# Transformer block on one core: second feed-forward product as one 512-column product per rows tile, with its sums in four PSUM banks

## The reference

```python
h = _layernorm(x, ln3_g, ln3_b)
p = h @ ff_w1 + ff_b1                       # 256 -> 2048
a, gate = (p[..., :D_FF], p[..., D_FF:])    # 1024 each
h = a * jax.nn.gelu(gate, approximate=False) @ ff_w2 + ff_b2
return h + x
```

## Time and profile before

| | us |
|---|---|
| median of 3 runs (lowest, highest) | 1708.18 (1707.97, 1708.85) |
| span of the profiled execution, first to last instruction | 1706.1 |
| PE busy in the span | 1697.1 (99%) |
| DVE busy | 1467.8 (86%) |
| ACT busy | 1186.1 (70%) |
| POOL busy | 1086.0 (64%) |

### The profile page before, as it was taken

The page is one execution under the profiler, slowest core; times in us unless marked ns, Lnnn a source line. Parts: engine busy times, 40 slices in busy tenths (PEclk is TensorE's granted clock), DMA queues, the critical chain, the costliest instruction groups (busy, mean ns, idle before and its releaser), DMA issues.

```text
span 1706.1 us, 42969 instructions
## 1 busy us (share of the span) xinstructions
PE 1697.1 (99%) x13628; PEld 1661.4 (97%) x13628; DVE 1467.8 (86%) x3184; ACT 1186.1 (70%) x3246; POOL 1086.0 (64%) x1812
## 2 busy tenths in 40 slices
PE   9999999999999999999999999999999999999999
PEld 8999999999999999999999999999999998888888
DVE  8888988888888888899999999999999998666665
ACT  7777777777777777777788877777877776222222
POOL 7787777766666666687777877777777666122211
PEclk9999999999999999999999999999999999999999
DMA  7777777676666566677777777776666663212110
GB/s 215 192 183 185 178 183 177 172 179 163 154 155 155 151 161 158 168 180 179 187 193 193 195 193 177 183 180 167 169 168 169 167 165 83 62 50 71 63 42 25
DMA packets 286432, 263.99 MB, mean 155 GB/s; under 512 B 102016, under 2 KB 246528, under 8 KB 286208
## 3 DMA queue, kind: packets, MB, share of 16 engines
q1 hardware_dynamic: 232416, 248.12, 57.0%
q10 hardware_dynamic: 53792, 13.12, 3.6%
HBM read 70.40 MB, written 24.90 MB: 56 GB/s over the span
## 4 chain that ended last, share of the span: by engine, by line
PE 96%; DVE 1%; POOL 1%; SPq 1%; DMA 1%; ACT 1%; issue 0%; ACTq 0%; POOLq 0%; DVEq 0%
PE QKB L356 20%; PE PVB L415 14%; PE PTB L370 13%; PE WOP L395 10%; PE VB L317 9%; PE S L304 7%; PE S L303 7%; PE PTB L944 5%; PE S L944 5%; PE QKB L960 3%; PE VB L960 3%; DMA PT<-in_L_xattn_sa_wq_dram 0%; DMA RX<-QKS 0%; ACT PT L522 0%; DVE NM L633 0%
## 5 line engine op out<-in xcount | busy, mean ns | idle before, releaser
L522 ACT ACTIVATE PT<-S,NM 128x256 f32<-128x256 f32 x1024 | 471.1, 472 | 180.6 <-DVE NM L633 179.8
L615 DVE TENSOR_TENSOR PL<-PTB,PH 128x512 fp32r<-128x512 f32 x512 | 349.7, 684 | 90.4 <-ACT PH L543 86.2
L835 POOL TENSOR_TENSOR ON<-ON,RB 128x256 f32<-128x256 f32 x256 | 188.4, 736 | 277.3 <-DVE ON L653 262.4
L543 ACT ACTIVATE PH<-PTB 128x1024 fp32r<-128x1024 f32 x256 | 263.2, 1028 | 102.0 <-PE PTB L370 98.6
L633 DVE TENSOR_REDUCE NM<-S 128x2 f32<-128x512 f32 x512 | 325.9, 677 | 0.2
L370 PE MATMUL PTB<-IDN,PT 128*128 128x128 f32 x2048 | 265.9, 273 | 0.2
L303 PE MATMUL S<-RX 128*128 128x256 f32 x1012 | 253.8, 283 | 0.0
L304 PE MATMUL S<-RX 128*128 128x256 f32 x1012 | 253.7, 283 | 0.0
L370 PEld LDWEIGHTS PTB<-IDN,PT 128*128 128x128 f32 x2048 | 229.5, 140 | 0.9 <-DVE PL L615 0.8
L395 PE MATMUL WOP<-WO,OT 128*128 128x256 f32 x1536 | 226.0, 283 | 0.0
L653 DVE TENSOR_TENSOR ON<-PVB,ON 64x256 f32<-64x256 f32 x512 | 213.3, 417 | 3.5
(11 more groups left out here) (145 smaller groups left out, 3141.5 us busy)
## 6 DMA issues: line engine op xcount, KB each, us to landing
RX<-QKS SPq DMA_DIRECT2D x506, 192.0 KB, 2.9
RX<-QKS SPq DMA_DIRECT2D x506, 128.0 KB, 2.8
RB<-denominators SPq DMA_DIRECT2D x512, 64.0 KB, 2.6
out_dram<-XR SPq DMA_DIRECT2D x32, 256.0 KB, 2.7
rows<-XN SPq DMA_DIRECT2D x24, 256.0 KB, 2.5
rows<-HF SPq DMA_DIRECT2D x23, 256.0 KB, 2.5
XR<-in_x_dram SPq DMA_DIRECT2D x16, 256.0 KB, 3.6
denominators<-RDT SPq DMA_DIRECT2D x256, 16.0 KB
```

Source lines behind the costliest of these rows:

```text
L522: last = e.activation(PT[:, c % 2, j * S:(j + 1) * S], S1[:, i, qt * S:(qt + 1) * S], ACT.Exp, bias=NM[:, j:j + 1], accum_out=DEN[:, c % 2 ...
L543: e.activation(PH[:, s % 2, :], PTB[:, :, :].rearrange("p i n -> p (i n)"), ACT.Copy) \
L615: e.tensor_tensor(PL[:, cols], PTB[:, i, :], PH[:, s % 2, cols].bitcast(F32), ALU.subtract).then_inc(a.dve_pl, 1)
```

## The change

In chunks 1 to 7 the first two passes of the second product become one: the stationary operand is the high gated rows, the moving operand the high and the low weights side by side (512 columns). The result is twice as wide, so each of the four row tiles has a whole bank: the left 256 columns hold the high sums, the right ones the low sums. The third pass (low rows, high weights) is added to the left 256. The four banks are the former `QKB`, `VB`, `PVB` and `WOP`, now slices of one tensor `OUTB`. Chunk 0 stays as it was. For each half VectorE makes two additions to the residual rows: left columns, then, after a wait for it, right columns.

```diff
-        QKB = pb("QKB", [P, 512])
-        VB = pb("VB", [P, 512])
+        OUTB = pb("OUTB", [P, 4, 512])
+        QKB, VB, PVB, WOP = (OUTB[:, n, :] for n in range(4))
         S1 = pb("S1", [P, 2, 512])
         PTB = pb("PTB", [P, 2, 512])
-        PVB = pb("PVB", [P, 512])
-        WOP = pb("WOP", [P, 512])
...
+        def w2_both(f):
+            return WA[:, 4 + f // 4, :, (f % 4) * D:(f % 4 + 1) * D]
...
                     if f == 0 and t % 2 == 0:
                         sl.wait(e, fs.dve_xo, s, 1, PAIRS // 2 if t == 0 else 0)
+                    if s >= PAIRS:
+                        if s == PAIRS and t == 0:
+                            e.wait_ge(a.dve_ad, ATT)
+                            e.wait_ge(a.dve_xo, 2 * B)
+                        if s == PAIRS and t == 1:
+                            e.wait_ge(fs.dve_xo, PAIRS)
+                        high, low = (FH[:, s % 2, hp, t * P:(t + 1) * P] for hp in range(2))
+                        e.matmul(OUTB[:, t, :].rearrange("p (w n) -> p w n", w=2), high, w2_both(f), start=f == 0,
+                                 stop=False, skip_group_check=True)
+                        last = e.matmul(OUTB[:, t, 0:D], low, w2(f, 0), start=False, stop=f == PAIRS - 1,
+                                        skip_group_check=True)
+                        continue
                     for n, (hp, wp) in enumerate(((0, 0), (0, 1), (1, 0))):
...
-                    e.tensor_tensor(XR[:, cols], OB[h][:, :], XR[:, cols], ALU.add) \
-                        .then_inc(fs.dve_xo, PAIRS // 2)
+                    if chunk == 1:
+                        e.tensor_tensor(XR[:, cols], OB[h][:, :], XR[:, cols], ALU.add) \
+                            .then_inc(fs.dve_xo, PAIRS // 2)
+                        continue
+                    x = XR[:, cols].rearrange("p (t n) -> p t n", t=TT)
+                    y = OUTB[:, TT * h:TT * (h + 1), :].rearrange("p t (w n) -> p t w n", w=2)
+                    e.tensor_tensor(x, y[:, :, 0, :], x, ALU.add).then_inc(fs.dve_xh, 1)
+                    e.wait_ge(fs.dve_xh, 2 * (chunk - 2) + h + 1)
+                    e.tensor_tensor(x, y[:, :, 1, :], x, ALU.add).then_inc(fs.dve_xo, PAIRS // 2)
```

More of the change, by code:

```diff
@@ L868, in __init__ @@
                 self.dve_xo = sem("dve_xo_f")
+                self.dve_xh = sem("dve_xh_f")
                 self.pl_ve = sem("pl_ve_f")
```

## The result

The changed kernel takes 1713.88 us (median of 6 runs, 1713.52 to 1714.93) against 1708.43 for the one before, measured beside it (6 runs): +5.4 us, ratio 1.0033, 95% interval 1.0021 to 1.0044, that is +3.6 to +7.5 us. It is slower by more than 0.2%, by a narrow margin at the lower end. The forecast was +3.3 and 1711.5, and its range ended at 1713.6. Of the 2.4 us between 1711.5 and 1713.88, 0.25 are the kernel before, which measures 1708.43 here and stood at 1708.18 when the forecast was made. The profiled execution has a span of 1712.3, 6.2 above before.

What follows compares the result with a forecast made beforehand. PE was taken as the bound, busy 99% and never waiting in the changed stretch. Merges -2.8, boundaries +4.9 and the end +1.2 sum to +3.3 on 1708.18, 1711.5 us, with an 8-in-10 range of 1709.0 to 1713.6.

Steps and rivals of the forecast that it cites:

- Merged products: In the second product, one 512-column product replacing two of 256 saves 0.013 us per tile, -2.8 us over 54 steps.
- I take 0.013, the value nearest to the steady rows: Saving per merge in us, near 0.227 against 0.239 from trace streams of 512-column and 256-column products.
- The lower bound: For the merged products: with all 512s at 0.231 to 0.236 us, the gain is 0.004 per merge, -0.9 in all.
- The sign that the prediction set for this term: The prediction falls if a slot inside a chunk isn't within 0.02 of 4.13 us.
- Chunk boundaries: At six boundaries, into chunks 2 to 7, PE stops 0.82 us for DVE's additions: +4.9 us, bounds +4.5 to +5.4.
- dependent DVE instructions follow each other 0.03 after the end: At a chunk boundary, the gap in us taken between each half's left addition and the right one waiting for it.
- The end: At the kernel's end, the last four additions chain and end later: +1.2 us, 1.0 to 1.4.
- No cost elsewhere: New bank addresses, semaphore, one-off waits and first boundary's extra waits cost nothing; no second delay on DVE.
- the merged product saves less than its share: Rival for the second product: at 0.004 us per merge the time is 1713.4, slower by over 0.2%; chance 0.16.
- The boundaries don't stop PE: Rival at chunk boundaries: no stop, 1706.6 us, chance 0.05; with the larger saving 1703.7, chance 0.04.
- the larger saving: Rival for the second product: merges save 0.020 us per tile and 0.026 per slot, -5.7, 1708.6 us; chance 0.18.

Runs made afterwards that it cites:

- experiment 3: Changed kernel without VectorE's second addition per half, so the right columns are left out in chunks 1 to 7: 1705.70 us, ratio 0.9990 against before.
- experiment 6: Changed kernel with a slot's four 512-column products first and its four 256-column ones behind, in 48 slots: 1712.89 us, ratio 1.0030 against before.
- experiment 7: Changed kernel with the wide product's moving operand as 512 neighbouring columns of high weights in place of high and low ones: 1713.55 us in one run.
- Experiment 5: Changed kernel with left columns of both halves added first, then right columns of both: 1711.69 us, ratio 1.0023 against before.
- experiment 2: Changed kernel with each wide product made as two products of 256 columns again: 1715.12 us, ratio 1.0039 against before.
- experiment 4: Changed kernel with the second product of a chunk's first step made later at six boundaries: 1707.26 us, ratio 0.9997 against before.
- experiment 8: Changed kernel with grouped second products, late ones at the boundaries, and the last chunk in the old form: 1705.59 us, ratio 0.9989 against before.
- experiment 1: Kernel before with only the PSUM bank addresses of the change: 1707.80 us, ratio 1.0002 against before.

## Why the prediction was wrong

The mechanism was right: a gain on every slot, a stop at six boundaries, and a longer end. Each of the three terms was sized too kindly, and the errors added up: +3.3 was forecast, and +5.8 is the sum of what they measured in the traces (+5.4 between the medians).

- **Merged products: -2.8 forecast, -1.8 measured** (experiment 3). The step that failed is "I take 0.013, the value nearest to the steady rows". The steady rows are of streams of one width, and the changed second product is none. Alternating, the wide products cost 0.227, 0.232, 0.241 and 0.236 and the narrow ones 0.113 to 0.120, a gain of 0.008 per merge. The lower bound named the right cause, the slow 512s behind 256s, and the prediction should have stood nearer to it. Experiments 6 and 7 settle that it is the alternation. The sign that the prediction set for this term, a slot within 0.02 of 4.13, held at 4.147 although a third of the gain was missing: it was too wide for a gain of 0.05. The warm gap of an isolated product, N / 2.4 + 2.5 ns in the Trainium skill ("TensorE: Matmul & The Clock Gate", "Back-to-back issue gap"), would make it 2.5 ns per merge. The trace doesn't agree: it shows 8 ns alternating and 13 grouped.
- **Chunk boundaries: +4.9 forecast, +6.2 measured.** A stop is 0.96 to 0.98 in place of 0.82 at five of six. What failed is "dependent DVE instructions follow each other 0.03 after the end". That row is of a rounding behind a multiplication; the addition behind an addition takes 0.10, twice per boundary, 0.14 of the up to 0.16. The kind of operation isn't what differs: the subtraction L1085, like the additions a TENSOR_TENSOR, follows the rounding that it waits for by 0.034 too. What differs is that the trace has a wait instruction of its own (L1102) ahead of the addition, 0.04 after the end of the one before, 0.02 long and 0.04 ahead of the addition, and none for the dependence at the other two. Experiment 5 removes the dependence and the gaps go. The stop left, at the third boundary, is 1.32: there the second L1103 starts 0.46 after the L1101 before it, at the same addition in the changed kernel and in experiments 2, 4, 6, 7 and 8. It isn't the dependence that takes longer: L1102 ends 0.06 after that L1101 as elsewhere (1576.39), and L1103 starts 0.40 later (1576.78). Experiment 5 shows no such hold, but there the wait instruction ends 0.45 ahead of the addition, which would hide one. What holds it is open.
- **The end: +1.2 forecast, +1.4 measured**: the same gap, twice.
- **No cost elsewhere** was right: the bank addresses (experiment 1), the extra waits at the first boundary, whose slot is 4.15, and DVE's next steps, which took the delay. Two of the six slots behind a stop are 4.18, 0.04 over a plain one, and three are 0.02 under it.
- Of the rivals, "the merged product saves less than its share" is what happened, though not alone: at 0.008 it gives -1.8 + 6.1 = +4.3, and the longer chain is the rest. "The boundaries don't stop PE" falls by the waits, the larger saving, which needed 4.07, by the slot of 4.147.

## What to carry to other kernels

Before a second reader is put on a buffer that TensorE wants back, read when it wants it: here two additions more were 1.4 us of an engine with slack, and cost 1.0 us of TensorE six times. Ask then whether TensorE has other work that can go ahead of the wait; moving one product behind the next step's first product took all six stops away. Price a changed instruction in the order in which it will stand: wide products among narrow ones gain 0.008 us per merge and grouped ones 0.013.

## What the runs showed of the hardware that was not expected

- A product of 512 columns right behind one of 256 goes in 0.232 to 0.241 ahead of the next; behind five or more of 512 it takes 0.227. Behind a run of twelve 256s the first five 512s take 0.233, 0.236, 0.229, 0.232 and 0.231 (kernel before). Whether the moving operand lies in one run or in two makes no difference (experiments 6 and 7).
- In the changed kernel an addition on VectorE that waits for the one before it, with the wait as an instruction of its own (L1102), starts 0.104 after its end in 13 of 14 places; a rounding that waits for a multiplication, without one, starts 0.034 after it. An addition that waits for nothing starts 0.08 before the end of the one ahead.
- One addition is held 0.35 us longer than its fellows, behind its wait instruction, at the same place in six kernels.
